# A four-layer decoder on one core: a load's wait moved to a later item, a store moved ahead of weight loads, a shorter inverse root

## The chip, the cores and the metric

The kernel runs on one core of one Trainium2 chip. The metric is device time in microseconds (us), the median over runs. It holds one launch, from the first load of the inputs to the store of the output.

## The reference

The input is `x`, 8 batches of 100 tokens of 256 features, and a context of 8 batches of 361 rows of 128 features. Four layers follow one another; each has self attention, cross attention to the context and a feed-forward part, each added to `x` and each fed by a layer norm of `x`. What matters here are four things:

```python
def _layernorm(x, axis=-1, eps=1e-05):
    m = jnp.mean(x, axis=axis, keepdims=True)
    v = jnp.var(x, axis=axis, keepdims=True)
    return (x - m) / jnp.sqrt(v + eps)
...
x = x + _L0_attn_ref(_layernorm(x), Wk, bk, Wv, bv, Wf, bf)        # 16 heads, values of 64, gelu after
x = x + _L0_xattn_ref(_layernorm(x), ctx_512, ctx_512, ...)         # and so on, 12 parts in all
...
# last part: a recurrence over the 100 tokens, whose input is xw = x @ gru_w_ih.T
def step(h, xw_t):
    hw = h @ gru_w_hh.T
    ...
    h_new = (1.0 - z) * n + z * h
_, hs = jax.lax.scan(step, h0, jnp.swapaxes(xw, 0, 1))
```

Everything is float32.

## The kernel before

The 12 parts are done in three streams, A (layer 0 and the attentions of layer 1), B (the attentions of layer 2) and C (those of layer 3), with the feed-forward parts of layers 1, 2 and 3 between and behind them. A stream is a list of items: one item is one batch in one part, so stream A has 40 items, the first 8 of kind "first" (self attention of layer 0). Each engine walks the same list, `for i in range(-3, items + 2)`, with four rounds `r` in each `i`, and the engines meet through semaphores only. TensorE is written ahead: in item `i` it makes keys, values and scores for item `i + 1`, and the weighted values of item `i - 1`.

**Start.** The sync engine (SP) issues all loads in one order: half of `x`, constants, the first weights (semaphore `l_wa0`), the other half of `x`, value and output weights (`l_wv`, `l_wf`), ten small loads (`l_small`, lines 2708 to 2717), the context (line 2719), and then the rest of weight pack WA, 5518 KB (line 2720, `l_wa`). GpSimd (POOL), once it has seen `l_wa`, makes two small tables for the cross attention of items 32 to 39 and raises `y_set` (lines 2625 to 2628). ScalarE (ACT) waits for `l_small`, `l_wa` and `y_set` ahead of item 0 (lines 1546 to 1549), VectorE (DVE) for `l_small` and `y_set` ahead of item 1 (lines 2022 to 2024). TensorE (PE) waits for `l_wf` and `l_small` ahead of item 1 and for `l_wa` ahead of item 6 (lines 1001 to 1008). In item 0 ACT's first work is the exponential of the scores (line 1496), which DVE has masked just before (line 1894); its bank is what TensorE needs for the second half of the scores (line 817).

**Norms.** `inverse_root` (line 1747) makes 1/sqrt(variance + eps) for four batches at once, on tiles of 100x4, by a bit trick and three Newton steps of four instructions each. `step` makes DVE wait for each of its own instructions. It is called at the start (line 2093) and by `norm_rest` (line 2107) at the ends of streams A, B and C. All other norms are split between `statistics` on DVE and `norm_group` on POOL, which have their own code.

**From stream C to the recurrence.** `xw` has 7 tiles of 128 tokens (the last has 32) by 3072 columns; after it come 7 tiles of `shown`, 1024 columns. Each tile is copied from PSUM by ACT and DVE into one of two halves of `xw_out` and stored by SP (`store_tile`). Tile `i` may be copied only when the store of tile `i - 2` has landed (`stored(i - 2)`, lines 1657 and 2270). Tiles 0 to 2 are made inside stream C (`drain_unit`), the others after it. Between the stores SP issues the recurrent weights `whh`, 28 loads of 384 KB (`load_whh`): 8 after `phase` reaches 4, then 5 behind each of the stores of tiles 3 to 6. SP issues in the order of its program; a wait in it holds back all that is behind it. The recurrence (line 1277) begins when the last tile of `shown` is copied.

Of the kernel before, what the change touches and what calls it, by code (L numbers as in the profile page):

```python
# [19 lines left out]
I32 = mybir.dt.int32  # L20
ACT = mybir.ActivationFunctionType
ALU = mybir.AluOpType
# [21 lines left out]
EPS = 1e-5  # L44
# [106 lines left out]
def build(nc, dram, out):  # L151
    with ExitStack() as ctx:
# [293 lines left out]
        def kind_of(ph, i):  # L446

            return KINDS[ph][i // B] if 0 <= i < B * len(KINDS[ph]) else None
# [17 lines left out]
        def items_of(ph):  # L466

            return B * len(KINDS[ph])
# [34 lines left out]
        def early_units(i, r):  # L503

            return {(38, 1): (0,), (38, 3): (1,), (39, 0): (2,), (39, 1): (3,), (39, 2): (4,), (39, 3): (5,), (40, 0): (6, 7)}.get((i, r), ())
# [872 lines left out]
        def _(act):  # L1378
# [87 lines left out]
            def keys_of(ph, i, c):  # L1466

                if kind_of(ph, i) == "whole":
                    dst, bias = k1[:, i % 2, c, :], wa("x_bk")[:, c:c + 1]
                else:  # L1470
                    dst, bias = mem[ph]["kX"][:, i % 3, c, :], yk[:, c:c + 1] if ph == "A" else kone[:, :]
                evacuate(dst, P, NK, ph, "kX", i, c, func=ACT.Identity, bias=bias)
# [36 lines left out]
            def row_exponentials(ph, i):  # L1509

                act.wait_ge(sem["peaks"], before(PEAKS, ph, i, 1))
                keys = NK if kind_of(ph, i) == "whole" else S
                nc.scalar.activation(P1[:, i % 2, 0:keys], banks[0:S, 0, 0:keys], ACT.Exp, bias=peak[:, i % 2:i % 2 + 1],
                                     accum_out=peak[:, 2 + i % 2:3 + i % 2]).then_inc(sem["sc_free"], 1)
# [23 lines left out]
            def stream(ph):  # L1538

                nc.scalar.preload_act_table(ACT.Exp)  # L1540
                for i in range(-3, items_of(ph) + 2):
                    if i == (-1 if ph == "C" else -3):
                        act.wait_ge(sem["set_done"], 1 + "ABC".index(ph))
                    now, then = kind_of(ph, i), kind_of(ph, i + 1)
                    past, later = kind_of(ph, i - 1), kind_of(ph, i + 2)
                    if ph == "A" and i == 0:
                        act.wait_ge(sem["l_small"], 16 * SMALL_LOADS)
                        act.wait_ge(sem["l_wa"], 32)
                        act.wait_ge(sem["y_set"], 1)
                    for r in range(4):  # L1550
                        if now in ("first", "band", "causal") and r < 2:
                            exponentials(ph, i, r)
                        if then in ("whole", "turned") and r == 0:
                            row_exponentials(ph, i + 1)
                        if now in ("whole", "turned") and r == 1:
                            exponentials(ph, i, 0)
                        if now == "cross":
                            exponentials(ph, i, 2 * r)
                        if later == "cross":
                            keys_of(ph, i + 2, r)  # L1560
                        if later == "whole" and r in (1, 2):
                            keys_of(ph, i + 2, r - 1)
                        if now == "cross":
                            exponentials(ph, i, 2 * r + 1)
                        for m in drain_units(i, r) if ph == "C" else ():
                            if m >= 11:
                                drain_unit(m)
                        if ph == "A" and (i, r) == (40, 0):
                            for m in early_units(i, r):
                                evacuate(early_h[:, m, :], P, HALF, "A", "shared", m, func=ACT.Gelu)  # L1570
                            for m in (4, 5):
                                _, _, evac_, value = unit_of(("A", "shared", m))
                                act.wait_ge(sem[evac_], value)
                            for m in range(6):
                                last = nc.scalar.activation(early_h[:, m, :], early_h[:, m, :], ACT.Gelu)
                            last.then_inc(sem["gelu"], 1)
                        if past == "turned" and r == 0:
                            u, evac_ = taken(ph, "pv", i - 1)
                            b = (i - 1) % B
                            nc.scalar.activation(XNT[:, :, columns_of(b)], u[:, 0:2 * S].rearrange("p (c q) -> p c q", c=C), ACT.Copy  # L1580
                                                 ).then_inc(sem[evac_], 1)
                        if kind_of(ph, i - 2) == "turned" and r == 1:
                            u, evac_ = taken(ph, "oR", i - 2)
                            b = (i - 2) % B
                            nc.scalar.activation(XNT[:, :, columns_of(b)], u[:, 0:2 * S].rearrange("p (c q) -> p c q", c=C), ACT.Copy
                                                 ).then_inc(sem[evac_], 1)
                        if then == "cross" and ph == "C" and r in (1, 2):
                            values_of(ph, i + 1, r - 1)
                        group_work(ph, i, r)
                        if past == "first" and r in (1, 2):  # L1590
                            half = r - 1
                            act.wait_ge(sem["divided"], 2 * (i - 1) + half + 1)
                            for c in range(4 * half, 4 * half + 4):
                                o_ = mem[ph]["oT"][:, columns_of(c)]
                                last = nc.scalar.activation(o_, o_, ACT.Gelu, bias=abv[:, c:c + 1])  # L1595
                            last.then_inc(sem["gelu"], 1)
                        if then in ("first", "turned") and r == 2:
                            own_values(ph, i + 1, 0)
                        if ph == "B":
                            wide_step(ph, i, r, 0)  # L1600
                            wide_step(ph, i, r, 1)
# [94 lines left out]
        def _(dve):  # L1696
# [3 lines left out]
            def step(ins):  # L1700

                steps[0] += 1
                ins.then_inc(sem["v_step"], 1)
                dve.wait_ge(sem["v_step"], steps[0])
# [41 lines left out]

            def inverse_root(y, x, t):

                step(nc.vector.tensor_scalar(x, x, EPS, None, ALU.add))
                step(nc.vector.tensor_scalar(y.bitcast(I32), x.bitcast(I32), 1, None, ALU.arith_shift_right))  # L1750
                step(nc.vector.tensor_scalar(y.bitcast(I32), y.bitcast(I32), -1.0, float(0x5F3759DF), ALU.mult, ALU.add))
                for _ in range(3):
                    if x.shape[1] == 1:
                        step(nc.vector.scalar_tensor_tensor(t, y, x, y, ALU.mult, ALU.mult))
                    else:
                        step(nc.vector.tensor_tensor(t, y, y, ALU.mult))
                        step(nc.vector.tensor_tensor(t, t, x, ALU.mult))
                    step(nc.vector.tensor_scalar(t, t, -0.5, 1.5, ALU.mult, ALU.add))
                    step(nc.vector.tensor_tensor(y, y, t, ALU.mult))

            def pick_two(nb, value, score):

# [253 lines left out]
            def stream(ph):  # L2016

                for i in range(-3, items_of(ph) + 2):
# [2 lines left out]
                    now, then, past = kind_of(ph, i), kind_of(ph, i + 1), kind_of(ph, i - 1)  # L2021
                    if ph == "A" and i == 1:
                        dve.wait_ge(sem["l_small"], 16 * SMALL_LOADS)
                        dve.wait_ge(sem["y_set"], 1)
                    for r in range(4):
                        if kind_of(ph, i - 2) == "first" and r == 0:
# [659 lines left out]
        def _(sp):  # L2686
# [210 lines left out]
            def load_whh(some):  # L2897

                for j, c, v in some:
                    ub = 4 * c + v  # L2900
                    sp.dma_start(arena[32 * j:32 * j + 32, 3072 * ub:3072 * ub + 3072], whh_rows[v, :, j, c, :]).then_inc(sem["l_whh"], 16)
# [14 lines left out]
            def store_drained(i):  # L2916

                for q in (4, 5):
                    _, _, evac_, value = unit_of(("C", "xw", i, q))
                    sp.wait_ge(sem[evac_], value)  # L2920
                store_tile(i)
# [23 lines left out]
            def load_expressions(lap, some):  # L2945

                for t in some:
                    sp.dma_start(expr[B * t:B * t + B], expr_rows[lap, t].rearrange("o b g -> (o b) g")).then_inc(sem["l_expr"], 16)

            load_whh(parts[0:8])  # L2950
            store_drained(2)
            sp.wait_ge(sem["ln"], norms_before("C", 2, 1) + 1)
            sp.dma_start(xn_rows.rearrange("(s b) d -> s (b d)", b=B), XN[:, :]).then_inc(sem["l_xnr"], 16)
            for i in range(DRAINED, 2 * TILES):
# [195 lines left out]
```

## Time and profile before

| | |
|---|---|
| median of 3 runs | 3190.74 us |
| lowest, highest | 3185.26, 3198.95 us |
| the profiled execution | 3187.26 us |
| its span (first to last instruction) | 3185.5 us |
| TensorE busy | 2958.3 us, 93% of the span |
| VectorE busy | 1555.2 us, 49% |
| ScalarE busy | 748.6 us, 24% |
| GpSimd busy | 290.2 us, 9% |

Every time of the trace counts from the start of the span. Busy TensorE is not TensorE at its peak: a multiplication at half the granted clock is busy for twice as long.

### The profile page before, as it was taken

To read this page: it belongs to the slowest core of one execution; us is meant where nothing else is said; L and a number is where in the kernel's file an instruction comes from. 1 tells how busy PE (TensorE), PEld (TensorE's weight loads), DVE (VectorE), ACT (ScalarE), POOL (GpSimd) and SP (SyncE) were. 2 spreads that over 40 slices of the span, in tenths; PEclk is the share of its full clock that TensorE was granted. 3 is DMA by queue.
4 is the path that set the end of the run, shared out by engine and by line. 5 is a ranking of instruction groups with operands and counts; after the bars stand their busy time and mean duration, and the time that the engine had idled before them with its cause. 6 is when DMAs were issued, how large, how long until landed. Compare 5 with 4: busy or idle time off the path is not lost.

```text
span 3185.5 us, 63821 instructions
## 1 busy us (share of the span) xinstructions
PE 2958.3 (93%) x25719; PEld 1663.0 (52%) x25719; DVE 1555.2 (49%) x4133; ACT 748.6 (24%) x1845; POOL 290.2 (9%) x681
## 2 busy tenths in 40 slices
PE   6888889899988999999889999999999999999997
PEld 4454456579755555555545643434444444444477
DVE  4545345411246566300475432466666666666653
ACT  2331124311122445311013421111111111111211
POOL 2112211020311010000311100000000000000011
PEclk9999989999988999999879999999999999999999
DMA  4000000078430000411000147000000001000076
GB/s 149 1 1 1 9 26 15 28 275 326 154 120 1 1 1 1 143 47 73 1 1 1 35 139 220 13 21 24 24 21 23 23 23 26 19 23 25 22 259 237
DMA packets 81362, 202.98 MB, mean 64 GB/s; under 512 B 32894, under 2 KB 56107, under 8 KB 68484
## 3 DMA queue, kind: packets, MB, share of 16 engines
q1 hardware_dynamic: 77208, 192.76, 18.5%
q0 software_dynamic: 3968, 7.56, 0.7%
q8 instruction: 140, 2.29, 0.3%
q14 instruction: 46, 0.38, 0.0%
HBM read 170.06 MB, written 37.53 MB: 65 GB/s over the span
## 4 chain that ended last, share of the span: by engine, by line
PE 81%; DVE 10%; ACT 3%; DMA 2%; issue 2%; POOL 1%; SPq 1%; DVEq 0%; POOLq 0%; ACTq 0%
PE banks L1277 32%; PE banks L1091 7%; PE banks L909 4%; PE banks L610 4%; PE banks L802 2%; PE banks L563 2%; PE banks L1324 2%; PE banks L1155 2%; PE banks L1167 2%; PE banks L931 2%; PE banks L1246 2%; PE banks L949 1%; PE banks L955 1%; PE banks L697 1%; PE banks L971 1%
## 5 line engine op out<-in xcount | busy, mean ns | idle before, releaser
L1277 PE MATMUL banks<-arena 128*32 128x384 f32 x12800 | 1034.3, 486 | 1.9 <-DVE arena L2282 1.1
L1277 PEld LDWEIGHTS banks<-arena 128*32 128x32 f32 x12800 | 416.6, 110 | 613.7 <-issue 610.0
L1668 ACT ACTIVATE arena<-arena 128x256 f32<-128x256 f32 x200 | 83.3, 416 | 759.4 <-DVE arena L2294 759.4
L2294 DVE TENSOR_TENSOR arena<-banks,arena 128x256 f32<-128x256 f32 x200 | 84.9, 424 | 199.8 <-PE banks L1277 198.5
L1091 PE MATMUL banks<-arena 128*128 128x400 f32 x512 | 172.5, 499 | 1.5 <-DVE arena L2245 0.8
L610 PE MATMUL banks<-XNT,arena 128*128 128x400 f32 x384 | 153.0, 541 | 9.7 <-ACT XNT L1400 3.7
L909 PE MATMUL banks<-arena 128*100 128x256 f32 x512 | 140.0, 428 | 14.0 <-ACT arena L1595 5.1
L1389 ACT ACTIVATE arena<-banks 128x512 f32<-128x512 f32 (+2 forms) x111 | 63.3, 570 | 353.2 <-PE banks L1155 143.4
L1091 PEld LDWEIGHTS banks<-arena 128*128 128x128 f32 x512 | 97.1, 190 | 76.8 <-DVE arena L2245 1.4
L1868 DVE TENSOR_REDUCE arena<-banks 100x4 f32<-100x1444 f32 x64 | 106.2, 1660 | 62.8 <-PE banks L758 62.6
L2574 POOL TENSOR_TENSOR rstd<-rstd 100x3 f32<-100x3 f32 (+1 forms) x120 | 23.3, 195 | 1233.5 <-DVE rstd L1823 1227.1
L802 PEld LDWEIGHTS banks<-arena 32*121 32x121 f32 x1536 | 100.7, 188 | 58.5 <-ACT arena L1502 35.6
L1502 ACT ACTIVATE arena<-banks 121x600 f32<-121x600 f32 x128 | 85.9, 671 | 182.6 <-PE banks L802 182.6
L2674 POOL DMA_INDIRECT region_rows<-arena x20 | 18.4, 922 | 1199.8 <-DVE arena L2423 1196.7
L1400 ACT ACTIVATE arena<-banks 128x361 f32<-128x361 f32 (+4 forms) x147 | 72.1, 491 | 233.0 <-PE banks L955 102.9
L909 PEld LDWEIGHTS banks<-arena 128*100 128x100 f32 x512 | 92.4, 188 | 52.0 <-issue 5.9
L802 PE MATMUL banks<-arena 32*121 32x100 f32 x1536 | 112.6, 279 | 6.2 <-ACT arena L1502 6.2
L610 PEld LDWEIGHTS banks<-XNT,arena 128*128 128x128 f32 x384 | 75.5, 204 | 69.4 <-issue 15.1
L563 PE MATMUL banks<-arena 128*100 128x256 f32 x448 | 100.2, 385 | 8.9 <-issue 4.8
L2298 DVE TENSOR_TENSOR arena<-arena,banks 128x128 f32<-128x128 f32 x200 | 57.7, 289 | 96.5 <-ACT arena L1668 96.5
L1091 PE MATMUL banks<-XNT,arena 128*128 128x400 f32 x288 | 102.0, 514 | 1.9 <-ACT arena L1389 0.9
L1934 DVE TENSOR_TENSOR X<-X,banks 100x256 f32<-100x256 f32 x56 | 23.5, 420 | 163.0 <-PE banks L911 100.2
(384 smaller groups left out, 4279.2 us busy)
## 6 DMA issues: line engine op xcount, KB each, us to landing
arena<-fc SPq DMA_DIRECT2D x22, 1024.0 KB, 4.7
arena<-pj SPq DMA_DIRECT2D x22, 1024.0 KB, 4.8
arena<-gu SPq DMA_DIRECT2D x21, 1024.0 KB, 5.0
arena<-whh SPq DMA_DIRECT2D x32, 384.0 KB, 10.9
arena<-dn SPq DMA_DIRECT2D x21, 512.0 KB, 5.9
arena<-xw SPq DMA_DIRECT2D x400, 24.0 KB
xw<-arena SPq DMA_DIRECT2D x6, 1536.0 KB, 7.3
arena<-hh SPq DMA_DIRECT2D x16, 512.0 KB, 3.2
```

Source lines behind the costliest of these rows:

```text
L563: last = nc.tensor.matmul(u[0:S, 0:cols], a, b, start=i == 0, stop=bias is None and i == len(parts) - 1)
L610: last = nc.tensor.matmul(u[:, 0:4 * S], w[:, kk], XNT[:, kk, columns_of(4 * g, 4)], start=kk == 0, stop=kk == C - 1)
L802: last = nc.tensor.matmul(banks[0:KR, 4 + jj, columns_of(kc)], m["kX"][r, i % 3, c, key_chunk(kc)], qA[r, c, columns_of(b)], start=True, s ...
L909: last = nc.tensor.matmul(u[0:S, 0:D], o_, w_, start=c == 0, stop=bias is None and c == len(parts) - 1)
L931: last = nc.tensor.matmul(u[0:S, 0:cols], XNT[:, kk, columns_of(b)], wa("f_w", C)[:, kk, 512 * j:512 * j + cols], start=kk == 0, stop=j < ...
L1091: last = nc.tensor.matmul(u[:, 0:HALF], w, x[:, half * HALF:(half + 1) * HALF], start=i == 0, stop=i == len(parts) - 1)
L1277: last = nc.tensor.matmul(banks[32 * j:32 * j + 32, 2 * c + i, 0:384].rearrange("p (g n) -> p g n", g=3), hT[:, 1 - i, 32 * ub:32 * ub + 3 ...
L1400: nc.scalar.activation(dst, u[0:rows, 0:cols], func, bias=bias, scale=scale).then_inc(sem[evac_], 1)
L1502: nc.scalar.activation(dst, banks[0:KR, 4:6, 0:KC * S], ACT.Exp).then_inc(sem["t_free"], 1)
L1668: nc.scalar.activation(rz[:, c, :], pre[:, c, :], ACT.Sigmoid).then_inc(sem["rz_done"], 1)
L1868: nc.vector.tensor_reduce(tops[:, c, 16:P:32], banks[0:S, 0:4, 0:NK], AX, ALU.max, negate=True).then_inc(sem["sc_free"], 1)
L2294: nc.vector.tensor_tensor(pre[:, c, :].rearrange("p (g n) -> p g n", g=2), banks[:, 2 * c + i, 0:2 * P].rearrange("p (g n) -> p g n", g=2) ...
```

## The change

Three edits.

1. The waits for `l_wa` (with its companion `y_set`) on ACT move from item 0 to item 4, and `l_small` there to item 1; on DVE `y_set` moves from item 1 to item 4.
2. SP waits for the copies of the third `xw` tile and stores it before it issues the 8 loads of `whh`; before, the loads came first.
3. `inverse_root` halves (variance + eps) in the instruction that adds eps, starts from a negative guess, and needs three instructions in each Newton step in place of four.

```diff
@@ ScalarE, stream
-                    if ph == "A" and i == 0:
+                    if ph == "A" and i == 1:
                         act.wait_ge(sem["l_small"], 16 * SMALL_LOADS)
+                    if ph == "A" and i == 4:
                         act.wait_ge(sem["l_wa"], 32)
                         act.wait_ge(sem["y_set"], 1)
@@ VectorE, inverse_root
-                step(nc.vector.tensor_scalar(x, x, EPS, None, ALU.add))
+                step(nc.vector.tensor_scalar(x, x, EPS, 0.5, ALU.add, ALU.mult))
                 step(nc.vector.tensor_scalar(y.bitcast(I32), x.bitcast(I32), 1, None, ALU.arith_shift_right))
-                step(nc.vector.tensor_scalar(y.bitcast(I32), y.bitcast(I32), -1.0, float(0x5F3759DF), ALU.mult, ALU.add))
+                step(nc.vector.tensor_scalar(y.bitcast(I32), y.bitcast(I32), -1.0, float(0x5F3759DF - 0x400000 - 2 ** 31), ALU.mult, ALU.add))
                 for _ in range(3):
-                    if x.shape[1] == 1:
-                        step(nc.vector.scalar_tensor_tensor(t, y, x, y, ALU.mult, ALU.mult))
-                    else:
-                        step(nc.vector.tensor_tensor(t, y, y, ALU.mult))
-                        step(nc.vector.tensor_tensor(t, t, x, ALU.mult))
-                    step(nc.vector.tensor_scalar(t, t, -0.5, 1.5, ALU.mult, ALU.add))
-                    step(nc.vector.tensor_tensor(y, y, t, ALU.mult))
+                    step(nc.vector.tensor_tensor(t, y, y, ALU.mult))
+                    step(nc.vector.tensor_tensor(t, t, x, ALU.mult))
+                    step(nc.vector.scalar_tensor_tensor(y, t, -1.5, y, ALU.add, ALU.mult))
@@ VectorE, stream
                     if ph == "A" and i == 1:
                         dve.wait_ge(sem["l_small"], 16 * SMALL_LOADS)
+                    if ph == "A" and i == 4:
                         dve.wait_ge(sem["y_set"], 1)
@@ SyncE
+            store_drained(2)
             load_whh(parts[0:8])
-            store_drained(2)
```

## Rows read from the trace of the kernel before

**Rows 1.** The page: the span.
```profile
span 3185.5 us, 63821 instructions
```
**Rows 2.** The chain that ended last, 0 to 140 us: start, us, what.
```profile
19.46 19.14 DMA arena<-WA
```
**Rows 3.** Timeline of ACT, item 0: start, us, instruction, idle before it and releaser.
```profile
40.94 0.84 ACT L1496 ACTIVATE arena<-banks 100x800 f32<-100x800 f32 x1 [8.70 <-POOL idle_g L2628]
```
**Rows 4.** Timeline of PE, around item 0.
```profile
29.64 3.68 PE L724 MATMUL banks<-arena,XNT 128*100 128x512 f32 x8
...
35.63 0.87 PE L752 MATMUL banks<-arena 32*100 32x100 f32 x30
41.83 1.66 PE L817 MATMUL banks<-arena 32*100 32x100 f32 x16 [5.33 <-ACT arena L1496]
43.41 5.46 PE L724 MATMUL banks<-arena,XNT 128*100 128x512 f32 x8
```
**Rows 5.** Timeline of DVE, around item 0.
```profile
35.84 1.00 DVE L1894 TENSOR_TENSOR banks<-banks,causalT 100x800 f32<-100x800 f32 x1 [1.05 <-PE banks L817]
...
46.30 1.82 DVE L1866 TENSOR_REDUCE arena<-banks 100x16 f32<-100x1600 f32 x1
48.92 0.69 DVE L1985 COPY arena<-banks 100x512 f32<-100x512 f32 x1 [0.79 <-PE banks L724]
```
**Rows 6.** Half microseconds: us, busy by engine, PEclk, DMA share, GB/s.
```profile
36.50:37.00 0.50, 0.00 (x0) 0.00 (x0) 0.34 (x1) 0.00 (x0) 0.44 (x2) 0.80 0.00 0
...
47.00:47.50 0.50, 0.50 (x3) 0.24 (x2) 0.50 (x1) 0.31 (x1) 0.00 (x0) 0.95 0.00 0
```
**Rows 7.** Timeline of DVE: the root at the start, and a three-operand instruction.
```profile
8.73 0.17 DVE L1758 TENSOR_SCALAR rstd<-rstd 100x4 f32<-100x4 f32 x1
8.93 0.16 DVE L1759 TENSOR_TENSOR rstd<-rstd 100x4 f32<-100x4 f32 x1
...
640.36 0.23 DVE L1777 SCALAR_TENSOR_TENSOR small<-small 100x64 f32<-100x64 f32 x1
```
**Rows 8.** Timeline of PE: the transposes that read each of the four norms.
```profile
12.26 1.57 PE L601 MATMUL banks<-const_sb,XN 100*128 100x100 f32 x8 [5.33 <-DVE XN L2095]
...
634.02 0.56 PE L555 MATMUL banks<-const_sb,XN 100*128 100x100 f32 x4 [0.23 <-DVE idle L1715]
...
1307.73 0.51 PE L555 MATMUL banks<-const_sb,XN 100*128 100x100 f32 x4
...
1889.18 0.57 PE L555 MATMUL banks<-const_sb,XN 100*128 100x100 f32 x4 [0.69 <-ACT arena L1400]
```
**Rows 9.** Timeline of SP's queue, 1878 to 1910 us.
```profile
1878.90 0.36 SPq L2908 DMA_DIRECT2D xw<-arena  x1
...
1879.64 5.35 SPq L2901 DMA_DIRECT2D arena<-whh  x8
1889.20 0.36 SPq L2908 DMA_DIRECT2D xw<-arena  x1
...
1902.42 0.35 SPq L2908 DMA_DIRECT2D xw<-arena  x1
```
**Rows 10.** Windows, columns as in rows 6; the last row is one long stretch.
```profile
1882.00:1883.00 1.00, 1.00 (x4) 0.46 (x3) 0.18 (x4) 0.26 (x1) 0.00 (x0) 1.00 1.30 393
1883.00:1884.00 1.00, 1.00 (x3) 0.38 (x2) 0.00 (x0) 0.60 (x1) 0.00 (x0) 1.00 0.91 197
...
1902.00:1903.00 1.00, 1.00 (x5) 0.24 (x3) 0.34 (x1) 0.00 (x0) 0.00 (x0) 1.00 0.68 287
...
1884.00:1955.00 71.00, 67.49 (x171) 26.51 (x169) 13.60 (x22) 11.26 (x21) 0.00 (x0) 1.00 1.01 276
```
**Rows 11.** The chain that ended last, 1860 to 1990 us.
```profile
1943.43 14.64 DMA shown<-arena
...
1958.74 12.26 PE banks L1246 x24
```
**Rows 12.** Timeline of ACT: its first copy of tile 4.
```profile
1909.72 0.60 ACT L1389 ACTIVATE arena<-banks 128x512 f32<-128x512 f32 x1 [9.19 <-PE banks L1246]
```

## The prediction

> **What bounds the kernel now.** I read the page first: a span of 3185.5 us [rows 1], nearly all of it a chain from one instruction to the next, TensorE's for the most part. Such a chain has no slack to lose, but each edit touches it in one spot only, so each is read from its own stretch. Second I read the chain over the first 140 us. For 19.14 us it runs through one transfer, the rest of pack WA [rows 2]; then POOL makes its two tables, and ACT starts item 0's exponential at 40.94, after 8.70 us of idleness that POOL's `y_set` ended [rows 3]. The work it waited to do had been ready since the mask of DVE was done. So the start is bound by a load that item 0 does not use. Third I read SP's queue and the DMA share around the end of stream C. From 1884 to 1955 us the DMA engines are full, share 1.01 [rows 10], and the chain then passes through a store of `shown` for 14.64 us, until 1958.07 [rows 11]. There the recurrence's start is bound by the amount of data that the DMA engines still have in front of them. Last I looked at who waits for the four roots [rows 8].
>
> **The change, part by part.**
>
> *The wait for the large load.* DVE's mask of item 0 runs from 35.84 to 36.84 [rows 5]. ACT would start the exponential some 0.04 us later, at 36.88, where it now starts at 40.94 [rows 3]: 4.06 us earlier. What else could hold item 0 or 1? The ten small loads and the output weights, which TensorE awaits ahead of item 1: they stand in the queue before the transfer of rows 2, which is over at 38.60, and TensorE is at item 1's weighted values no sooner than 44 us (now past 48.92, when their value copy starts [rows 5], less the 4.9 won below). So that wait is met. The moved waits for `l_wa` and `y_set` now stand ahead of item 4: the load is over at 38.60 and `y_set` comes before 40.94, when the engines are still in item 0, so they cost nothing, and neither does what is queued behind them.
>
> The clock could add to this. TensorE ends its scores at 36.50 and is idle for 5.33 us [rows 4]; the granted clock falls at once, to a mean of 0.80 in 36.50 to 37.00, and returns to full in 47.00 to 47.50 [rows 6]. The two levels are 1.2 and 2.4 GHz. At the low one the eight records of L724 took 5.46 us, where the same took 3.68 at the high one; L817 took 1.66, against 0.87 for the like-sized L752 [rows 4]. If the clock did not fall, the chain would win 0.79 on L817 and, on L724, no more than the 0.80 us by which DVE waited (its reduction ended at 48.12, the value copy began at 48.92, rows 5): 1.6 at most. Below, nothing: TensorE will still be idle from 36.50 to about 37.8, and the clock fell within the first half microsecond of that gap. I take the middle, 0.8, since the low stretch would start while less work is left to meet it. First edit: 4.06 + 0.8 = 4.9 us gained, between 4.1 and 5.7.
>
> The Trainium skill, page "TensorE: Matmul & The Clock Gate", section "Part 1: The HAM clock gate (the "warmup" mystery)", says that the monitor behind this clock runs freely, so that the same kernel meets a different number of slow multiplications from run to run. By that rule no gain of the clock should be counted on and the sum would keep 4.1; by the rows alone it might keep 5.7.
>
> *The shorter root.* Instructions of the root start 0.20 us apart, at 8.73 and 8.93 [rows 7]. Three fewer in a call: 0.6 us. The new instruction has three operands. On 100x4 the trace has none; the one on 100x64 takes 0.23 against 0.16 and 0.17 for those replaced [rows 7], so each could cost up to 0.06 more, and a call wins 0.4 to 0.6. I take 0.6, as 4 columns are nearer to 4 than to 64. It counts where somebody waits. At the start TensorE waits 5.33 us for the norm [rows 8]: all 0.6, now that the chain goes through item 0 and no longer through the load. At the end of A TensorE waited 0.23 us [rows 8]: 0.2. At the end of B it had no idle time before its transposes, and at the end of C it waited for ACT's copy [rows 8]: nothing; if the cover by TensorE's own work were gone, 0.6 each. Sum 0.8 us gained, between 0.4 and 2.4.
>
> *The store ahead of the weights.* This one I expect to cost. Now SP issues the second tile's store at 1878.90, from 1879.64 the eight `whh` loads, and at 1889.20 the third tile's store, as soon as its last copy is done [rows 9]. That time does not move: it hangs on ACT and TensorE. With the new order SP stands at that wait with the eight loads behind it, and they can start only after 1889.6. What do the DMA engines do meanwhile? The second store runs at 393 GB/s until about 1883.4, then the rate falls to 197, the pace of the weights [rows 10]. So from 1883.4 to 1889.7 (issue at 1889.20 takes 0.36 us [rows 9], and I allow 0.5 to the first bytes) the engines would have nothing: a pause of 6.3 us, from 5.7 to 6.7 by which part of the row at 1883 is store. From there to 1955 they are full, 1.01 over 71 us [rows 10], so nearly all of the pause is handed on. Where they have room they take some back: the emptiest microsecond is 1902 to 1903 at 0.68 [rows 10], just as the fourth tile's store is issued at 1902.42 [rows 9]; I allow 0.5 us in all. The `shown` store that ends the wait at 1958.07 [rows 11] then lands 5.8 us later, and the last 12.26 us of multiplications [rows 11] with it.
>
> What does the earlier store buy? Tile 4 may be copied once it has landed. ACT's first copy of tile 4 was released by TensorE, not by a store [rows 12], so nobody was waiting: nothing. The stores of tiles 4 and 5 also land some 6 us later, and copies of tiles 6 and 7 may wait, but TensorE has four banks to run ahead in and the last word is still the queue's; I count nothing more. Third edit: 5.8 us lost, between 4 and 7.
>
> *Sum.* -4.9 - 0.8 + 5.8 = +0.1 us. The profiled execution, 3187.26 us (span 3185.5 [rows 1] and 1.8 around it), becomes 3187.4. That execution is 3.5 us below the median of 3190.74, so on the scale of the median: 3190.8, say 3191.
>
> **The rivals.** 0.5% is 16 us, about what a measurement of this kernel can tell from no change; the three runs of before are 13.7 us apart.
>
> *Rival 1, the pause is hidden (0.15).* If the weights ran beside the stores without slowing them, the order would not matter and 5.7 us would be won: 3185. For it: the mean of 276 GB/s over the 71 us [rows 10] lies well above the weights' 197, so the engines can move more than weights alone do. Against it: a share of 1.01 at that mean leaves no room, and stores at 393 between weights at 197 explain it.
>
> *Rival 2, the queue runs dry again (0.15; slower).* The late landings of tiles 4 and 5 hold back copies, these hold back the next stores, and each of those has five weight loads behind it in SP's program. Then the DMA engines pause a second time, before the store of tile 5 or 6. The pause of the first kind costs 6.3; a second of the same size, and the clock falling once more for the 1.8 us that L724 showed, gives 5.8 + 6.3 + 1.8 - 5.7 = +8: 3199. It decides once a tile's store is issued after the five loads before it are done. A round of SP brings 4.0 us of store (1536 KB at 393 GB/s) and 10.0 us of weights (five times 384 KB at 197), 14 us together. Against it: since the 71 us stayed full [rows 10], the rounds now come faster than that, and the backlog grows from round to round; after the change it is larger by the pause.
>
> *Rival 3, the first edit does nothing (0.05).* If something else held item 0 until 41 us, only the roots' 0.2 and the loss of 5.8 would be left: 3196. Nothing in rows 2 to 5 does.
>
> *Rival 4, the clock (0.05).* Moving the first items against the clock's falls could add or take a fall in several of them. At 1.8 us a fall, and some five to ten in stream A, up to 16 us in either direction.
>
> **How the numbers follow.** The likeliest, at 0.6, is the sum: 3191. Its own range, from the bounds (-5.7 - 2.4 + 4 = -4 and -4.1 - 0.4 + 7 = +2.5), is 3187 to 3193. Rivals 1 and 2 reach from 3185 to 3199, and the run-to-run spread widens that: 3182 to 3200. None of the cases but the last passes 16 us, with the spread on top: faster 0.05, same 0.89, slower 0.06.
>
> **What would show it.** In the profile after: ACT's first L1496 at about 36.3 us, released by DVE; TensorE's next L817 4 to 5 us earlier; nine root instructions after the guess where there were twelve; SP's third store at the issue time of before (moved only by what was won ahead), eight loads behind it, and a DMA share near zero for 6 us ahead of it; the first `shown` store landing 74.7 us after the third store's issue, where it was 1958.07 - 1889.20 = 68.9. The prediction is wrong if that last distance stays at 69 (rival 1) or passes 80 (rival 2), or if the start gains less than 3 us.

## The result, and the profile after

The changed kernel takes 3199.02 us, median of 20 executions (3189.65 to 3218.00), where the kernel before takes 3189.46 on the same chip (20 executions, 3184.47 to 3198.95). The ratio is 1.0031, 95% interval 1.0021 to 1.0041: slower by 9.6 us, or by 0.3%. That is within the bound of 0.5% and inside the range, and 8 us above the likeliest time. The signs of both halves came out as forecast; the size of one and something outside both did not.

**The start.** Three views of the kernel after, in the stretch of [rows 3, 4 and 6]: the timeline of ACT, the timeline of PE, and half microseconds (columns as in rows 6).

```profile
35.73 0.84 ACT L1496 ACTIVATE arena<-banks 100x800 f32<-100x800 f32 x1 [4.63 <-DVE banks L1891]
```
```profile
36.62 0.95 PE L817 MATMUL banks<-arena 32*100 32x100 f32 x16 [1.26 <-ACT arena L1496]
37.50 3.68 PE L724 MATMUL banks<-arena,XNT 128*100 128x512 f32 x8
```
```profile
36.50:37.00 0.50, 0.39 (x8) 0.39 (x10) 0.00 (x0) 0.06 (x1) 0.00 (x0) 1.00 0.01 0
...
47.00:47.50 0.50, 0.50 (x14) 0.50 (x16) 0.50 (x1) 0.00 (x0) 0.00 (x0) 1.00 0.00 0
```

The exponential now waits for DVE's mask and starts 5.21 us earlier (40.94 before). TensorE's idleness ahead of L817 has shrunk from 5.33 us to 1.26, and the granted clock stays full, so L817 takes 0.95 and the eight records of L724 take 3.68 where they took 1.66 and 5.46 [rows 4].

**The root.** Timeline of DVE at the start: nine instructions, 0.20 us apart, of which the first three and the last are shown, then the first user of the result.

```profile
8.09 0.16 DVE L1754 TENSOR_TENSOR rstd<-rstd 100x4 f32<-100x4 f32 x1
8.29 0.17 DVE L1755 TENSOR_TENSOR rstd<-rstd,stats 100x4 f32<-100x4 f32 x1
8.49 0.16 DVE L1756 SCALAR_TENSOR_TENSOR rstd<-rstd 100x4 f32<-100x4 f32 x1
...
9.69 0.16 DVE L1756 SCALAR_TENSOR_TENSOR rstd<-rstd 100x4 f32<-100x4 f32 x1
9.89 1.38 DVE L2093 TENSOR_SCALAR XN<-X,stats,rstd 100x256 f32<-100x256 f32 x4
```

On 4 columns the instruction of three operands takes 0.16 us, no more than those that it replaces. The user starts at 9.89, where before it started at 10.73. Of the 0.84 us, 0.6 are the three instructions. The other 0.24 are not won by the edit: in this execution the statistics began 0.29 earlier (5.53 for 5.82), and the instruction that adds eps, which now also halves, took 0.27 for 0.21.

**The store ahead of the weights.** First SP's queue at the same place as [rows 9], then single microseconds and one long stretch (columns as in rows 10).

```profile
1897.22 0.33 SPq L2906 DMA_DIRECT2D xw<-arena  x1
1897.60 5.73 SPq L2899 DMA_DIRECT2D arena<-whh  x8
...
1910.43 0.36 SPq L2906 DMA_DIRECT2D xw<-arena  x1
```
```profile
1890.00:1891.00 1.00, 1.00 (x4) 0.48 (x3) 0.00 (x0) 0.28 (x1) 0.00 (x0) 1.00 0.93 393
1891.00:1892.00 1.00, 1.00 (x3) 0.38 (x2) 0.00 (x0) 0.60 (x1) 0.00 (x0) 1.00 0.48 201
1892.00:1893.00 1.00, 1.00 (x4) 0.46 (x3) 0.00 (x0) 0.00 (x0) 0.00 (x0) 1.00 0.00 0
...
1897.00:1898.00 1.00, 0.56 (x4) 0.37 (x4) 0.00 (x0) 0.52 (x3) 0.00 (x0) 1.00 0.00 0
...
1970.00:1971.00 1.00, 0.00 (x0) 0.00 (x0) 0.00 (x0) 0.00 (x0) 0.00 (x0) 1.00 0.68 180
...
1897.20:1973.50 76.30, 65.01 (x160) 25.28 (x160) 13.61 (x22) 9.35 (x18) 0.00 (x0) 0.96 0.98 269
```

The same long stretch of the kernel before, from the issue of the third store to the landing of the first `shown` store:

```profile
1889.20:1958.10 68.90, 62.98 (x160) 24.78 (x160) 13.61 (x23) 9.47 (x19) 0.00 (x0) 0.98 1.00 280
```

And the chain that ended last, after, which answers to [rows 11]:

```profile
1937.33 16.64 DMA xw<-arena
...
1954.76 18.77 DMA shown<-arena
...
1974.20 12.34 PE banks L1246 x24
...
1987.60 12.44 PE banks L1277 x149
```

The second store ends near 1891.5; SP stands at the third store's wait until 1897.22, the eight weight loads behind it, and the DMA engines do nothing for some 6.5 us. The first `shown` store lands at 1954.76 + 18.77 = 1973.53, that is 76.3 us after the third store's issue, where it was 68.9: 7.4 us later, with 5.8 forecast. The two long rows account for it. Before, 68.9 us at 280 GB/s are 19.3 MB; after, 76.3 us at 269 are 20.5 MB. The 1.2 MB between them are what the DMA engines used to move ahead of the third store's issue (6.3 us at 197 GB/s is 1.24 MB). By the shares, the engines' busy time rose from 68.9 to 74.8 us (76.3 times 0.98), so 5.9 us, almost the forecast, are the weights' own time; the other 1.5 are time in which the engines were not full. 0.8 us of it pass until the first bytes come (share 0 up to 1898). In the last three microseconds, of which the row at 1970 shows the first, the mean share is 0.59, where it was 0.86 in the kernel before: 0.8 us more. The shares have two decimals, so the split is good to some 0.7 us. I had allowed 0.5 us of room to be won back; none was.

The chain also shows a wait that the kernel before did not have. The copy that feeds the first `shown` store now stands behind the store of the sixth `xw` tile (issued at 1937.33, landed 16.64 us later), where before TensorE was what it followed. The `shown` store is so issued 57.5 us after the third store, where it was 54.2, and takes 18.77 us to land in place of 14.64.

**Where the profiled execution lost the rest.** Its span is 3200.4 us, 14.9 above the one before. The first L909 comes 6.1 us earlier than before (66.25 for 72.33), but stream A ends only 1.5 us earlier, stream C ends 8.0 us later, and the recurrence starts 15.5 us later. Between those two points, where the profiled execution lost 9.5 us, the edits have changed only the roots at the ends of A and B; the mean granted clock from 1580 to 1860 us is 0.86, and 0.89 before. The experiments below come back to this.

### The profile page after: what moved, and what is told of

The parts are those of the page before. It is cut to its first block, busy times and chain, and to the rows that moved or that the text cites. A ratio compares the mean times of both kernels' runs of the same rounds, so it can differ in the third digit from the quotient of the medians.

```text
span 3200.4 us, 63809 instructions
## 1 busy us (share of the span) xinstructions
PE 2975.5 (93%) x25719; PEld 1673.8 (52%) x25719; DVE 1554.0 (49%) x4121; ACT 748.5 (23%) x1845; POOL 290.5 (9%) x681
## 4 chain that ended last, share of the span: by engine, by line
PE 81%; DVE 10%; ACT 3%; DMA 2%; issue 2%; POOL 1%; SPq 0%; DVEq 0%; POOLq 0%; ACTq 0%
PE banks L1277 32%; PE banks L1091 7%; PE banks L610 4%; PE banks L909 4%; PE banks L563 3%; PE banks L802 2%; PE banks L1324 2%; PE banks L1155 2%; PE banks L1167 2%; PE banks L931 2%; PE banks L949 1%; PE banks L955 1%; PE banks L1246 1%; PE banks L971 1%; PE banks L697 1%
## 5 line engine op out<-in xcount | busy, mean ns | idle before, releaser
L1277 PE MATMUL banks<-arena 128*32 128x384 f32 x12800 | 1034.3, 486 | 1.9 <-DVE arena L2280 1.1
L1277 PEld LDWEIGHTS banks<-arena 128*32 128x32 f32 x12800 | 416.6, 110 | 613.7 <-issue 608.9
L909 PE MATMUL banks<-arena 128*100 128x256 f32 x512 | 145.0, 439 | 14.9 <-ACT arena L1596 5.4
L909 PEld LDWEIGHTS banks<-arena 128*100 128x100 f32 x512 | 94.6, 192 | 55.2 <-issue 7.3
L563 PE MATMUL banks<-arena 128*100 128x256 f32 x448 | 102.3, 390 | 9.9 <-issue 4.9
```

The lines of the kernel that those rows point to most:

```text
L563: last = nc.tensor.matmul(u[0:S, 0:cols], a, b, start=i == 0, stop=bias is None and i == len(parts) - 1)
L909: last = nc.tensor.matmul(u[0:S, 0:D], o_, w_, start=c == 0, stop=bias is None and c == len(parts) - 1)
L1277: last = nc.tensor.matmul(banks[32 * j:32 * j + 32, 2 * c + i, 0:384].rearrange("p (g n) -> p g n", g=3), hT[:, 1 - i, 32 * ub:32 * ub + 3 ...
```

## The experiments

The theory: two independent parts, a gain of some 6 us at the start and a loss of some 7 us in the DMA queue at the end of stream C. Its rivals: the loss lies elsewhere (the root, or the moved waits), or the parts act on each other, or the clock's falls belong to the change. Ratios are to the kernel before on the same chip, with 95% intervals; the first four kernels shared one chip and 30 executions of the kernel before (median 3188.56).

**The store alone.** The kernel before, with the two calls in the new order:

```diff
+            store_drained(2)
             load_whh(parts[0:8])
-            store_drained(2)
```

> The third tile's store ahead of the eight weight loads, nothing else changed. If the loss sits in the DMA pause: the first store of shown lands 75 to 77 us after the issue of the third store where it was 68.9, the recurrence starts 90 us after that issue where it was 82.9, and the time is 6 to 8 us over the kernel before. If the loss comes from the earlier start (the clock's falls meeting other items): no change, within 2 us.

Measured: 3194.20 us, ratio 1.0021 (1.0010 to 1.0032), so 3 to 10 us slower. The chain of this kernel:

```profile
1943.21 18.98 DMA shown<-arena
...
1962.87 13.67 PE banks L1246 x24
```

The third store is issued at 1885.92 and `shown` lands at 1962.19: 76.3 us, just as in the whole change. The last multiplications take 13.67 instead of 12.26 us [rows 11]: the granted clock is at 0.50 for their first 6 us, where in the kernel before it had that level for their first 3. So the recurrence starts 8.8 us later in all. The loss belongs to this edit by itself.

**The waits alone.** The kernel before, with the waits on ACT and DVE moved:

```diff
-                    if ph == "A" and i == 0:
+                    if ph == "A" and i == 1:
                         act.wait_ge(sem["l_small"], 16 * SMALL_LOADS)
+                    if ph == "A" and i == 4:
                         act.wait_ge(sem["l_wa"], 32)
...
+                    if ph == "A" and i == 4:
                         dve.wait_ge(sem["y_set"], 1)
```

> The moved waits alone. By the sum of the prediction 4 to 6 us less. If the clock gives back what the start wins, as the trace of the changed kernel suggests (6.1 us ahead at item 1, 1.4 ahead from 384 us on): the first L1496 at 36.9 us, but the total between 3 us less and 3 us more than before. If the loss of the whole change comes from here: 5 to 10 us more.

**The root alone.** The kernel before, with the nine-instruction root:

```diff
                     step(nc.vector.tensor_tensor(t, t, x, ALU.mult))
-                    step(nc.vector.tensor_scalar(t, t, -0.5, 1.5, ALU.mult, ALU.add))
-                    step(nc.vector.tensor_tensor(y, y, t, ALU.mult))
+                    step(nc.vector.scalar_tensor_tensor(y, t, -1.5, y, ALU.add, ALU.mult))
```

> The shorter root alone. At the start the chain still goes through the large load, so only the 0.2 us at the end of stream A is left: within 1 us of before. If the three-operand instructions cost more than they save, up to 2 us more.

**Waits and root together**, without the store.

> All but the store's move. By the queue's pause as the cause of the loss: the stretch from the third store's issue to the start of the recurrence is 82.9 us as before, and the time is 7 to 8 us below the whole change, 0 to 6 below the kernel before. If the first and third edits lose by the clock: above the kernel before.

Measured: waits alone 3184.15, ratio 0.9989 (0.9979 to 0.9998); root alone 3188.14, 0.9999 (0.9988 to 1.0010); both 3181.87, 0.9977 (0.9966 to 0.9987), so 4 to 11 us faster. ACT's first exponential, in the kernel with the root alone:

```profile
42.23 0.84 ACT L1496 ACTIVATE arena<-banks 100x800 f32<-100x800 f32 x1 [11.49 <-POOL idle_g L2624]
```

and with the waits alone:

```profile
36.36 0.84 ACT L1496 ACTIVATE arena<-banks 100x800 f32<-100x800 f32 x1 [4.64 <-DVE banks L1895]
```

As long as item 0 waits for the load, a shorter root buys nothing, ACT only idles longer (11.49 us for 8.70, of which 1.3 come from the load, which ended that much later in this execution); with the waits moved, the start is at 36.36, and with both at 35.29. The release by DVE's mask shows that nothing else holds item 0.

**The whole change again, a smaller dose, and two kernels without the slow weights.** These four ran on another chip, with 35 executions of the kernel before (3186.17). The first is the changed kernel itself.

> The whole change once more, beside kernels of one chip. If the parts simply add (waits and root 7.3 us less, the store's move 6 to 9 more): within 3 us of before. If the whole change is slower than its parts add up to, as its first timing of 1.0031 says against a sum near 1.000: 6 to 13 us more than before.

Measured: 3189.69, ratio 1.0009 (0.9991 to 1.0027). The recurrence again starts 91.7 us after the end of stream C.

The second puts the store between four loads and four:

```diff
-            store_drained(2)
-            load_whh(parts[0:8])
+            load_whh(parts[0:4])
+            store_drained(2)
+            load_whh(parts[4:8])
```

> Waits and root as in the change, but four of the eight weight loads issued ahead of the third tile's store and four behind it. If the cost of the store's move is the pause of the DMA engines: four loads at 2.0 us each fill it (1883.4 to 1891), so the stretch from the third store's issue to the start of the recurrence is 82.7 us as without the move, and the time is that of waits and root, 5 to 8 us below before. If the cost comes from the store being ahead of weights as such: half of it or all of it stays, 3 to 9 us on that stretch.

Measured: 3183.55, ratio 0.9986 (0.9971 to 1.0001). SP's queue and two microseconds, ahead of the third store's issue and just behind it:

```profile
1876.12 3.43 SPq L2899 DMA_DIRECT2D arena<-whh  x4
1885.67 0.36 SPq L2906 DMA_DIRECT2D xw<-arena  x1
1886.07 3.62 SPq L2899 DMA_DIRECT2D arena<-whh  x4
```
```profile
1883.00:1884.00 1.00, 1.00 (x4) 0.44 (x3) 0.00 (x0) 0.60 (x1) 0.00 (x0) 1.00 0.93 197
...
1886.00:1887.00 1.00, 0.74 (x7) 0.42 (x5) 0.00 (x0) 0.67 (x3) 0.00 (x0) 1.00 1.02 209
```

Four loads (1.5 MB) fill the gap, the DMA engines never stop, and the start of the recurrence is back at 84.5 us from the end of stream C. So it is the pause that costs, and not the order of store and weights.

The third has waits and root, the old order, and `whh` laid out so that each load of 384 KB writes all 128 partitions, 3 KB each, and no longer 32 partitions with 12 KB each:

```diff
-                for j, c, v in some:
-                    ub = 4 * c + v
-                    sp.dma_start(arena[32 * j:32 * j + 32, 3072 * ub:3072 * ub + 3072], whh_rows[v, :, j, c, :]).then_inc(sem["l_whh"], 16)
+                for part, c, v in some:
+                    at_ = 3072 * (4 * c + v) + 768 * part
+                    sp.dma_start(arena[:, at_:at_ + 768], dram["whh"][:, at_:at_ + 768]).then_inc(sem["l_whh"], 16)
```

> Waits and root, store order as before; the recurrent weights lie in DRAM in the order of the partitions, and each load writes 768 columns of all 128 partitions in place of 3072 columns of 32. Same bytes, same count of loads. If the pace of 197 GB/s comes from writing 32 partitions: the pace goes to the stores' 393, the backlog at the end is gone, the wait of 5.9 us on the store of shown with it, and the time is 5 to 9 us below waits and root alone. If the pace comes from the reads or the size of a load: nothing changes.

Measured: 3175.81, ratio 0.9972 (0.9955 to 0.9989). SP's queue, single microseconds, and the chain of this kernel:

```profile
1870.22 5.53 SPq L2898 DMA_DIRECT2D arena<-whh  x8
...
1893.01 0.33 SPq L2905 DMA_DIRECT2D xw<-arena  x1
```
```profile
1877.00:1878.00 1.00, 1.00 (x3) 0.38 (x2) 0.00 (x0) 0.59 (x1) 0.00 (x0) 1.00 1.05 421
...
1891.00:1892.00 1.00, 1.00 (x3) 0.19 (x1) 0.00 (x0) 0.13 (x1) 0.00 (x0) 1.00 0.00 0
```
```profile
1899.80 54.09 PE banks L1246 x125
...
1954.96 20.18 PE banks L1277 x245
```

At the same share of about 1 the weights now move at 421 GB/s instead of 197 (400 to 424 in the microseconds of 1875 to 1880, in which nothing else moves). The engines even run dry ahead of the fourth tile's store (share 0.00 at 1891) and it costs nothing: the chain has no transfer in it any more, TensorE runs from 1899.80 to the recurrence without waiting for a store. The recurrence starts after 76.5 us, 7.5 less than with waits and root alone. The Trainium skill, page "SBUF — State Buffer", section "Door 1: The DMA port swizzle (why `[64,N]` ≈ `[32,N]`)", states that partitions 0 to 31 reach only 8 of the 16 ports. The trace agrees as far as it can: 197 GB/s for loads that each write 32 partitions, 400 to 424 for loads that write 128. That the ports are the reason is the page's word; this experiment also changed the length of a partition's row and the order in DRAM.

The fourth is the third with the store ahead of the eight loads.

> As the kernel with weights to all partitions, and the third tile's store moved ahead of the eight loads as in the change. If the move costs only through a backlog that is handed on: with no backlog it costs nothing, within 1 us of that kernel on the stretch from the third store to the recurrence. If it costs by anything else: 5 to 9 us more on that stretch.

Measured: 3177.05, ratio 0.9972 (0.9958 to 0.9986); 76.4 us. Where the queue has no backlog, the edit that cost 7.5 us costs nothing.

**Do the parts add up?** The halves give 0.9977 times 1.0021 = 0.9998, within 0.0015, and the whole had given 1.0031. So whole and halves were timed together, with the loads to all partitions alone as a fourth, on the chip of the halves' first timing, against 35 executions of the kernel before (3200.84, where the same chip had 3188.56 before).

> The whole change, beside its two halves on one chip. If the parts add: the product of the two halves' ratios, 1.0000 within 0.0015, and in the trace 91.7 us from the last L680 to the recurrence. If they don't add, as the first timing says: 1.002 or more over that product.

> The first half of the change again: 0.9965 to 0.9985, 84.0 us from the last L680 to the recurrence. The stretch from 1010 us to the last L680 took 868.8 us in its first trace and 874 to 875 in four kernels with both halves. If the clock's falls there are chance, either value can come; if they hang on the program, 868.8 again.

> The store's move again: 1.0015 to 1.0030, and 91.7 to 93.0 us from the last L680 to the recurrence. On the stretch before it, as for the kernel above: 868.9 again if it hangs on the program, either value if it is chance.

> The kernel before with the weights written to all partitions, and nothing else. If the gain is that of the removed backlog: 76.5 us from the last L680 to the recurrence where it was 84.2, and a ratio near 0.9977 (7.6 us). If it needed the other edits: 84 us and 1.000.

Measured: whole 3220.89, 1.0036 (1.0006 to 1.0066); waits and root 3210.82, 1.0008 (0.9979 to 1.0037); store alone 3207.03, 1.0012 (0.9986 to 1.0039); loads to all partitions alone 3191.93, 0.9977 (0.9949 to 1.0005). The executions here spread over 30 us and more, and those of the whole and of waits and root fall into two groups (whole: 3195 to 3202, and 3216 to 3230), so the medians say little of 7 us. The product of the halves is 1.0020 here, within 0.004, and the whole's 1.0036 agrees with it as well as with a loss beyond them.

Each execution's mean granted clock is on record too, and it accounts for nearly all of the spread: among the 35 of the kernel before, a clock lower by 0.001 goes with a time longer by 2.9 us, and what that leaves is 2.4 us (standard deviation, of 9.9). So the kernels can be compared at the same mean clock, by one straight line for all executions of a timing, as differences in us to the kernel before:

| timing | whole | waits and root | store alone |
|---|---|---|---|
| first four kernels | | -6.4 (1.8) | +6.5 (1.6) |
| second four, other chip | +0.2 (2.0) | | |
| last four kernels | -0.9 (1.9) | -7.0 (1.8) | +5.5 (1.8) |

In brackets stands half of the 95% interval. At the same clock the halves add up, and the whole costs nothing. The whole's own mean clock was lower than that of the kernel before: 0.9606 for 0.9621 on the second chip, where that difference is within noise, and 0.9552 for 0.9591 in the last timing, where it is not. At 2.6 and 3.0 us for each 0.001, the slopes of these two timings, that is 4 and 12 us, which is all that the whole lost there. The line has a limit: what an edit does through the clock is counted as clock. The waits alone come out at -1.0 (1.6) by it, at a mean clock 0.0008 above that of the kernel before. So it shows where the whole's loss sits, and not whether the change brings the lower clock about. In the first timing of the whole (mean clock 0.9591) it can't be drawn, as only one execution of the kernel before has its clock on record there.

The traces show in which stretches the time went. Three distances of each profiled execution, worked out from first and last instructions of a line: stream C without its ends (first L949 to last L680), from there to the recurrence (first L1277), and the start of L1107 at the end of stream A.

| kernel | L1107 starts at | stream C | to the recurrence |
|---|---|---|---|
| before | 628.7 | 868.9 | 84.2 |
| after | 627.2 | 874.3 | 91.7 |
| whole again | 620.6 | 875.1 | 91.7 |
| whole, third time | 621.6 | 887.0 | 91.8 |
| store alone | 628.8 | 868.9 | 93.0 |
| store alone, again | 625.6 | 887.8 | 93.2 |
| waits alone | 621.1 | 869.0 | 84.0 |
| root alone | 629.9 | 868.9 | 84.2 |
| waits and root | 622.7 | 868.8 | 84.0 |
| waits and root, again | 629.2 | 869.0 | 84.2 |
| four loads, store, four | 622.6 | 874.4 | 84.5 |
| all partitions, waits and root | 622.5 | 868.9 | 76.5 |
| the same, store first | 623.4 | 875.2 | 76.4 |
| all partitions alone | 632.6 | 887.9 | 76.5 |

The last column follows the order of store and weights and their partitions: 7.5 to 7.8 us for the store ahead of the loads where waits and root are in, 8.8 and 9.0 where it stands alone, none without a backlog. The middle column is not fixed by the program: the store alone took 868.9 us once and 887.8 the other time. Yet the whole change had 874 to 887 in each of its three traces, and waits and root 869 in both of theirs. In all fourteen, the value is above 870 in six of the seven traces that have the store ahead of some or all of the eight loads, and in one of the other seven, although the edit is first reached at the end of that stretch. Against a link speaks the mean clock of all executions: with the store first and the loads to all partitions it was 0.9621, that of the kernel before, and with the old order of the same two 0.9614. The runs don't decide whether this is chance.

**What moves the middle column.** First one and the same program, the store alone, in its two traces. Windows of the one with 868.9, and of the one with 887.8:

```profile
1697.00:1724.00 27.00, 25.42 (x308) 18.11 (x312) 13.39 (x20) 11.79 (x21) 3.89 (x14) 1.00 0.01 1
```
```profile
1702.70:1719.80 17.10, 17.10 (x82) 10.89 (x74) 3.96 (x4) 4.41 (x7) 0.00 (x0) 0.50 0.00 0
...
1730.00:1740.20 10.20, 10.20 (x46) 6.95 (x47) 2.66 (x4) 1.90 (x3) 0.00 (x0) 0.50 0.00 0
```

The same eight matmuls of L758 start at 1697.16 in the one and at 1702.40 in the other, 5.2 us later; at those that start at 1723.70 and 1741.78 the lag has grown to 18.1. So 12.8 of the 18.9 us come about here, in two stretches at half the clock.

Then two kernels that run the same code there, the one with loads to all partitions and the same with the store first. One line of each one's PE timeline, and the nine microseconds behind it. With the old order:

```profile
1775.01 0.87 PE L758 MATMUL banks<-arena 32*100 32x361 f32 x8 [0.79 <-DVE arena L1865]
```
```profile
1777.00:1786.00 9.00, 9.00 (x82) 6.24 (x82) 4.34 (x9) 4.25 (x8) 3.17 (x13) 1.00 0.01 2
```

With the store first:

```profile
1775.67 1.51 PE L758 MATMUL banks<-arena 32*100 32x361 f32 x8 [0.80 <-DVE arena L1865]
```
```profile
1777.00:1786.00 9.00, 9.00 (x41) 6.34 (x36) 2.60 (x4) 1.90 (x3) 0.00 (x0) 0.50 0.00 0
```

After the same idleness of 0.8 us, the same instruction runs at the high level of 2.4 GHz in one execution, while in the other the clock falls to the low one of 1.2 GHz as it starts, and stays there for some ten microseconds; TensorE gets through half as many matmuls (41 for 82). The two executions are 0.66 us apart ahead of it; the next L758 starts at 1780.82 in the one and at 1786.33 in the other, so this fall cost 4.9 us. The Trainium skill, page "TensorE: Matmul & The Clock Gate", section "Part 1: The HAM clock gate (the "warmup" mystery)", says that the monitor runs freely and that the same kernel meets a different number of slow multiplications from run to run; the two traces of the store alone agree (868.9 and 887.8 us).

## Why the prediction was right, and where it was off

The two mechanisms that the sum is made of were right. That the total still lies inside the range, by 1 us, is owed to the width that a rival gave it, and so in part to luck.

- **The wait for the load.** Mechanism as forecast: released by DVE, start at 35.73 for about 36.3. The term was 4.9 us, and 5.7 with the root. In the profile after, the exponential came 5.2 us earlier and the clock did not fall, so the first L909 came 6.1 earlier, 0.3 of which came with `x`: near the upper end (5.7 and 0.6 for the root), not the middle. Timed with the root, the pair gave 6.7 us (3181.87 for 3188.56) with an interval of 4 to 11. The second timing of the pair, 0.9979 to 1.0037, neither supports nor excludes that by itself; at the same mean clock it is 7.0 us faster.
- **The root.** 0.6 us at the start, with the three-operand instruction at 0.16 us, the cheap bound. Alone it won nothing (0.9999), because the load then covered it.
- **The store ahead of the weights.** This term was mis-sized. Forecast +5.8 us, from a pause of 6.3 less 0.5 of room. Measured +7.4 at the landing of `shown`, and +7.5 to +7.8 at the start of the recurrence. The pause itself and its handing on were right (5.9 us of DMA time); no room was won back, and 1.5 us more were lost in time when the queue was not full, ahead of the first bytes and while the last store thinned out. I had also counted nothing for copies that wait for the later stores; in the profile after, one that waits for the sixth `xw` store stands in the chain, so the last word was not the queue's alone. How much of the 1.5 us is due to it is not shown. Alone, the edit costs 1.4 us more, through the clock (13.67 us for 12.26). The bound of 7 was too low.
- **The sum.** With the terms as measured it would be -5.7 or -6.1 and +7.5, so +1 to +2 us, and the halves' ratios multiply to 0.9998. The whole measured 1.0031, 1.0009 and 1.0036. The first lies above that product even with the halves' own intervals (0.0015) added; the second and the third don't settle it, the third having halves of its own with 1.0020. The missing term is the clock in the streams, which the sum put at nothing outside item 0. At the same mean clock the whole costs +0.2 and -0.9 us, which is the sum of the forecast; what it lost beyond that in these two timings goes with its lower mean clock. In the profiled execution it lies in stream C, which took 5.4 us longer, and in the stretches before it. Whether the change makes the falls more frequent, or the timings only happened to fall so, stays open.
- **The rivals.** Rival 1, the pause is hidden, falls: share 0.00 up to 1898, and 76.3 us for 68.9. Rival 2 named 3199, the time that was measured, but that is luck: its first step is there, a copy held back by a late store, but the second pause is not (share 0.98 over the 76.3 us, and the distance stayed below 80). Rival 3, the first edit does nothing, falls with 35.73 and with the waits alone. Rival 4, the clock, makes up the rest of the total, as the comparison at the same mean clock shows for two of the three timings. I gave it 0.05. I counted its falls in stream A alone, where stream C has them too, and at 1.8 us each, where one measured 4.9; their number in stream A I had not read from rows.
- **The scale.** That both parts lie below 0.3% and of opposite sign, so that the total stays within 0.5%, held for the ratio of every timing (the interval of the whole's third reaches 0.66%).

The version that beats both kernels is the one with loads to all partitions, waits and root: 0.9972 (0.9955 to 0.9989), some 9 us faster than the kernel before.

## What to carry to other kernels

Ahead of a store that has to wait for its data, put enough transfers into the same queue to last until the data are there (here four loads of 384 KB did); all that stands behind the store is late by the pause wherever the queue stays full until the end. Before arguing over the order of a full queue, read bytes beside share: here a share of 1 at 197 GB/s, where other transfers reached 393, pointed at the shape of the transfer, and changing that took the whole wait away. And a total of two small parts of opposite sign is only as good as the clock's spread: time each part, compare distances between the same instructions, and compare executions at the same mean granted clock.

## What the hardware showed that was not expected

- Loads of 384 KB into 32 partitions moved at 197 GB/s with the DMA engines at a share of 1; the same bytes into 128 partitions moved at 400 to 424 GB/s, although each partition's row was then a quarter as long.
- The granted clock after one and the same 0.8 us of idleness stayed at the high level in one execution and was at the low one for some ten microseconds in another, 4.9 us for that fall. Stream C took 869, 874 to 875, or 887 to 888 us in fourteen executions, the same program 868.9 and 887.8.
- In the last three microseconds before the first `shown` store landed, the DMA share was 0.68, 0.62 and 0.60 with the whole change, and 0.86 on average in the kernel before.
- The mean granted clock of an execution accounts for nearly all of the difference between executions of one kernel: 2.9 us for each 0.001 in the last timing, and of a standard deviation of 9.9 us it leaves 2.4.
